# A six-bank ring with paired maxima in place of a seven-bank ring with single maxima, in the second layer's attentions

## The reference

```
def _attn(x, ctx, wq, wk, wv, wo, bo, num_heads):      # 16 heads of 16 columns
    q, k, v = ...                                      # projections
    scores = jnp.einsum('bthd,bshd->bhts', q, k) / np.sqrt(hd)
    p = jax.nn.softmax(scores, axis=-1)
    o = jnp.einsum('bhts,bshd->bthd', p, v)
x = _attn(_ln(x), _ln(x), ...) + x        # self1: 512 keys
x = _ffn(_ln(x), ...) + x
x = _attn(_ln(x), context, ...) + x       # cross1: 1601 keys
x = _ffn(_ln(x), ...) + x
```

## Time and profile before

| | |
|---|---|
| median of 3 runs | 3810.48 us (3810.12 to 3816.46) |
| the profiled execution's own time | 3808.21 us |
| its span | 3806.4 us |
| granted TensorE clock, mean over the span | 0.921 |
| a2, from its first maxima to its last values | about 2454 to 2655 us of the span |
| a3, the same | about 3015 to 3590 us |

### The profile page before, as it was taken

One profiled execution on the slowest core, in us unless ns is written; L12 is line 12 of the kernel. 1 busy time (PEld: TensorE's weight loads), 2 busy tenths in 40 slices (PEclk: granted clock), 3 DMA queues, 4 the chain that ended last, 5 costly groups with the idle time before them and its releaser, 6 DMA issues. The chain is left out here.

```text
span 3806.4 us, 50843 instructions
## 1 busy us (share of the span) xinstructions
PE 3285.1 (86%) x17084; PEld 1868.4 (49%) x17084; DVE 2259.6 (59%) x4090; ACT 1817.3 (48%) x3349; POOL 1081.7 (28%) x538
## 2 busy tenths in 40 slices
PE   7978886899799999999997778598678599999776
PEld 5734443778644444444443566333466344444255
DVE  4356664434266666666663454397444499999333
ACT  4434443444334444444444233177344178888733
POOL 0045653000047777777776000012000000000000
PEclk8978997999889999999998899799799699999888
DMA  5877775999966666666661341233463523222210
GB/s 207 279 182 192 188 191 195 310 326 308 291 159 150 148 149 150 149 150 149 148 150 49 139 155 55 83 119 119 170 193 109 154 90 102 97 88 100 82 67 38
DMA packets 364812, 588.04 MB, mean 154 GB/s; under 512 B 47042, under 2 KB 200226, under 8 KB 363470
## 3 DMA queue, kind: packets, MB, share of 16 engines
q1 hardware_dynamic: 363632, 582.64, 52.1%
q10 hardware_dynamic: 958, 2.62, 0.4%
HBM read 341.51 MB, written 240.88 MB: 153 GB/s over the span
## 5 line engine op out<-in xcount | busy, mean ns | idle before, releaser
L1493 ACT ACTIVATE a_prob<-a_ring 128x512 f32<-128x512 f32 (+1 forms) x1088 | 577.8, 600 | 664.9 <-PE a_ring L1413 624.8
L1517 DVE TENSOR_REDUCE a_blk_max<-a_ring 128x1 f32<-128x402 f32 x1024 | 519.7, 568 | 328.9 <-PE a_ring L1397 328.7
L1092 ACT ACTIVATE a_prob<-a_ring 128x512 f32<-128x512 f32 (+1 forms) x1088 | 582.1, 605 | 97.1 <-PE a_ring L1012 92.5
L1363 POOL TENSOR_TENSOR a_prob_sum<-a_prob,a_prob_sum 128x1024 f32<-128x1024 f32 x256 | 599.4, 2380 | 3.8 <-ACT a_prob L1493 3.8
L1435 PE MATMUL a_pv<-a_prob,a_v 128*64 128x512 f32 (+1 forms) x2176 | 545.4, 621 | 0.0
L1137 DVE TENSOR_REDUCE a_blk_max<-a_ring 128x1 f32<-128x402 f32 x1024 | 507.1, 568 | 63.8 <-PE a_ring L999 57.0
L1412 PE MATMUL a_ring<-a_q_stack,a_k_stack 128*128 128x512 f32 (+1 forms) x1088 | 468.6, 431 | 53.2 <-issue 38.4
L1413 PE MATMUL a_ring<-a_q_second,a_k_second 65*128 65x512 f32 (+1 forms) x1088 | 441.9, 406 | 0.0
L1363 POOL TENSOR_TENSOR a_prob_sum<-a_prob 128x1024 f32<-128x1024 f32 x128 | 301.9, 2369 | 453.6 <-DVE a_chunk_sum L1548 244.2
L1030 PE MATMUL a_pv<-a_prob,a_v 128*32 128x256 f32 (+2 forms) x4096 | 340.7, 406 | 13.6 <-ACT a_prob L1092 7.8
L742 DVE TENSOR_TENSOR p_split_lo<-p_ps,p_split_hi 128x512 fp32r<-128x512 f32 (+2 forms) x280 | 171.4, 622 | 302.6 <-ACT p_split_hi L630 299.8
(11 more groups left out here) (252 smaller groups left out, 4660.0 us busy)
## 6 DMA issues: line engine op xcount, KB each, us to landing
a_k_stack<-k_hi_cross SPq DMA_DIRECT2D x96, 400.5 KB, 4.6
a_v<-v_cross SPq DMA_DIRECT2D x48, 768.0 KB
a_k_stack<-k_lo_cross SPq DMA_DIRECT2D x80, 400.5 KB, 6.0
a_k_second<-k_hi_cross SPq DMA_DIRECT2D x32, 801.0 KB, 12.5
v_cross<-p_v_sb SPq DMA_DIRECT2D x48, 512.0 KB, 4.1
k_hi_cross<-p_split_hi SPq DMA_DIRECT2D x120, 200.0 KB, 3.3
k_lo_cross<-p_split_lo SPq DMA_DIRECT2D x120, 200.0 KB, 3.4
a_q_stack<-q_hi_self SPq DMA_DIRECT2D x64, 256.0 KB, 4.1
```

The source lines that it names most:

```text
L1092: nc.scalar.activation(prob[0:keys, tau % RC, m, :], ring[0:keys, score_place(e) % BANKS, :], ACT.Exp, scale=a.scale).then_inc(exp_done, 1)
L1363: nc.gpsimd.tensor_tensor(prob_sum[:, h], prob_of(i * NCP + cp, h), other, ALU.add)\
L1493: nc.scalar.activation(prob_of(w, h)[0:keys, ch % 2, :], ring[0:keys, score_bank(e), :], ACT.Exp, scale=a.scale).then_inc(exp_done, 1)
L1517: nc.vector.reduce_max(dst, ring[:, max_bank(g), 0:a.blk], AX.X).then_inc(item_read, 1)
```

## The change

VectorE takes both blocks of a pair by one instruction: it reads two neighbouring banks (two runs of 402 or 512 values in each partition) and writes two maxima. It starts when both products have landed, and marks both as read when it ends. For the two banks of a pair to be neighbours wherever the ring has come to, the ring has six banks in place of seven. The eighth bank of PSUM goes to the values as before, and one bank is now unused.

```diff
@@ -773,7 +773,7 @@
-    BANKS = 7
+    BANKS = 6
@@ -1129,13 +1129,14 @@
             def blocks(g0, g1):
-                for g in range(g0, g1):
-                    i, j, t, nb, r = item_of(g)
-                    c = 8 * r + 4 * j + t
-                    dst = blk_max[:, i % 2, c, nb:nb + 1] if NB > 1 else row_max[:, i % 2, c:c + 1]
-                    dve.wait_ge(item_done, g + 1)
-                    nc.vector.reduce_max(dst, ring[:, item_place(g) % BANKS, 0:a.blk], AX.X).then_inc(item_read, 1)
-                    if g % NI == NI - 1:
+                for g in range(g0, g1, 2):
+                    i, j, t, nb, _ = item_of(g)
+                    c, n = 4 * j + t, item_place(g) % BANKS
+                    dst = blk_max[:, i % 2, c:c + 9:8, nb] if NB > 1 else row_max[:, i % 2, c:c + 9:8]
+                    dve.wait_ge(item_done, g + 2)
+                    nc.vector.reduce_max(dst, ring[:, n:n + 2, 0:a.blk], AX.X).then_inc(item_read, 2)
+                    if g % NI == NI - 2:
                         turn(i)
```

## The result

The changed kernel takes 3878.5 us (median of 4 runs, 3871.7 to 3884.75) against 3810.96 for the kernel before on the same chip (3810.12 to 3816.46). The ratio is 1.0174 [1.0154, 1.0194]: slower by 67.5 us where 48 were forecast. The profiled execution took 3879.94 us.

A forecast was written before the change was run, and what follows sets the result against it. It took TensorE as slightly the tighter in a3, with VectorE right beside it, and VectorE as the bound in a2. Terms 50 - 4 + 2 gave 48 us more, 3858 us, range 3834 to 3882.

The forecast's parts named there:

- the walk: Hand timing of ring waits in both attentions; four a3 half-units go from 5.04 to 5.58 us, a2's loop takes 2.73.
- Six banks, a3: In a3's units, maxima and scores wait for banks held by exponentials: 50 us more, bounds 42 and 61.
- VectorE's own part in the ring is no limit in a3: In a3, maxima's banks are free about 1.4 us behind their product, scores need them 2.0 or more behind: no cost.
- Six banks, a2: In a2's units, VectorE stays the bound and the unit goes from 2.87 to 2.91 us: 2 us more.
- the once-a-group work: In a2, VectorE's 1.6 us a group comes in two lumps, of which 0.7 a group sticks out.
- One reduction for two: VectorE's paired reduction takes 983 or 1211 ns, saving 0.067 or 0.069 us a pair; only the starts count, 4 us less.
- the 4 us at the starts: Ahead of each attention's first unit, where only VectorE limits, 42 and 18 pairs save 4 us.
- VectorE's time is what counts: Rival: the ring has room, so less VectorE work speeds both attentions: 34 us less, 3776; faster has chance 0.10.
- TensorE hides the late load: Rival: in a3 the maxima's new wait of 0.38 us costs only 0.07, total 3810; no change has chance 0.04.
- The clock: Rival: stalls draw the clock to 0.50 for a tenth of a3, 50 us on top, 3908; chance 0.05.
- a2's unit was to stay within 0.1 of 2.87 us: Sign in a2: the time per unit should hardly move, staying within 0.1 of 2.87 us.
- The maxima's load was to wait for ScalarE: Sign in a3: the maxima's weight load waits for ScalarE several times the earlier 25.3 us of 480.

The follow-up runs named there:

- e1: Kernel before, with six ring banks in place of seven and single reductions kept: 3876.7 us against 3811.0, ratio 1.017.
- e4: Changed kernel, with ScalarE computing only 256 of 512 columns of each a3 exponential, so the output differs: 3840.1 us (one run).
- e5: Kernel before, with ScalarE computing only 256 of 512 columns of each a3 exponential, so the output differs: 3806.0 us (one run).
- e2: Changed kernel, with seven banks in place of six; pairs whose banks are not neighbours are read by two reductions: 3837.1 us, ratio 1.006.
- e7: Kernel before, but both banks of a pair are marked as read only by the second single reduction: 3843.7 us (one run).
- e6: Kernel before, but the first single reduction of a pair waits for both products: 3812.5 us (one run).
- e9: Changed kernel, with the values of a group's first chunk multiplied in two halves of the columns: 3861.8 us, ratio 1.0127.
- e8: Kernel before, with the values of a group's first chunk multiplied in two halves of the columns: 3807.0 us against 3811.8, ratio 0.9977.
- e10: e8 with paired reductions only ahead of each attention's first unit, seven banks, single ones where the ring wraps: 3803.0 us, ratio 0.9968.

## Why the prediction was right, and where it was not

**The number.** 3878.5 us lies 20 us above the 3858 forecast and near the upper end of the range. The spans differ by 71.8 us, 24 more than forecast, and the traces put 11.5 us of this excess in a2, 2.6 in the starts, 1.8 in a3, and 7.3 ahead of a2, where nothing was changed and only scatter stands. That a3 came so close, 51.8 against 50, is partly luck: the ring alone, which the walk was about, costs 43.8, at the lower end of its 42 to 51, and 8.0 more (e1 to after) came from a step that the prediction had put at nothing.

**Six banks, a3 (predicted +50).** The mechanism held. A round of four half-units that starts with one of two pairs takes 5.58 us in e1 (mean of 32 rounds away from the undivided values) and 5.62 after, where it took 5.07 before; the walk had 5.58 and 5.04. Two plain ones in a row take 2.67 in both, where it had 2.62. The timeline of e1, from a half-unit with two pairs to the next, shows its last step:

```profile
3205.79 0.18 PEld L1012 LDWEIGHTS a_ring<-a_q_stack,a_k_stack 64*128 64x128 f32 x2 [0.41 <-DVE a_blk_max L1137]
...
3207.19 0.51 PEld L1012 LDWEIGHTS a_ring<-a_q_stack,a_k_stack 64*128 64x128 f32 x2 [0.41 <-ACT a_prob L1092]
```

The second load of that row starts 0.18 us ahead of its end, at 3207.52, which is 1.73 us behind 3205.79 as forecast. But the first load, from which half-units are counted, needs only the first exponential and stands at 1.40. So with single reductions those with two pairs take 1.40 and the one behind them 1.54, and not 1.73 and 1.18; the walk had given the whole wait to the first of them. The number of units in 400 us, 141, VectorE's share (84.7%, said 82), ScalarE's (78%) and the clock came as forecast. That this loop hangs on the exponentials is shown by e4 and e5 for the kernel after (27.5 us of 51.8); for e1 alone no run shortened them, and it rests on the row above and the walk.

**The failed step in a3 is "VectorE's own part in the ring is no limit in a3".** It looked at the scores that need the bank of a pair of maxima 2.0 us behind, and overlooked the second pair of maxima of a half-unit with two: with six banks it needs the pair three earlier, and its own slot is only about 1.38 us behind that (1.18 for a half-unit and 0.2 for the first pair). Paired, these banks are free 0.48 + 1.00 + 0.05 = 1.53 us behind their products' start, as in e4's row of 3201.39. In the single form the first bank came back about half a microsecond sooner. With seven banks this is worth 18.1 us (e2), of which e7 gives 13.5 to the late release and e6 1.7, near its scatter, to the late start; the 3 us between them and e2 (the paired start's 0.065 us, the wrap of the ring) were not taken apart. Ring and pairs don't add: 43.8 and 18.1 apart, 51.8 together. That fits delays that overlap, as the half-unit behind one with two pairs takes 1.45 us in e1 and 1.34 after, but no run takes it apart.

**Six banks, a2 (predicted +2, bounds -8 and +14; measured +13.7).** Score products in 120 us fell from 167 to 154, so the unit takes 3.12 us where 2.91 was forecast. The groups of a2 after, 2500 to 2620 us:

```profile
L1138 DVE TENSOR_REDUCE a_row_max<-a_ring 128x2 f32<-128x1024 f32 x78 | 91.3, 1209 | 15.3 <-PE a_ring L999 15.3
...
L1012 PE MATMUL a_ring<-a_q_stack,a_k_stack 64*128 64x512 f32 x154 | 37.4, 481 | 17.7 <-DVE a_row_max L1138 17.7
```

VectorE, which the walk kept as the bound, waits 15.3 us of 120 for products, while the scores' products wait 17.7 for VectorE. That is a loop between the two and not a load on one. The timeline of a2 after shows it:

```profile
2562.36 1.06 PE L1030 MATMUL a_pv<-a_prob,a_v 128*32 128x512 f32 x8
2563.36 0.50 PE L999 MATMUL a_ring<-a_k_stack,a_q_stack 63*128 63x512 f32 x2
2563.69 0.40 PE L1012 MATMUL a_ring<-a_q_stack,a_k_stack 64*128 64x512 f32 x2
2563.93 0.40 PE L999 MATMUL a_ring<-a_k_stack,a_q_stack 63*128 63x512 f32 x2
...
2563.99 2.36 DVE L1138 TENSOR_REDUCE a_row_max<-a_ring 128x2 f32<-128x1024 f32 x2 [0.98 <-PE a_ring L999]
...
2565.27 0.50 PE L1012 MATMUL a_ring<-a_q_stack,a_k_stack 64*128 64x512 f32 x2 [0.94 <-DVE a_row_max L1138]
...
2566.28 0.51 PE L999 MATMUL a_ring<-a_k_stack,a_q_stack 63*128 63x512 f32 x2
...
2566.92 1.23 DVE L1138 TENSOR_REDUCE a_row_max<-a_ring 128x2 f32<-128x1024 f32 x1 [0.57 <-PE a_ring L999]
...
2568.20 0.50 PE L1012 MATMUL a_ring<-a_q_stack,a_k_stack 64*128 64x512 f32 x2 [0.18 <-DVE a_row_max L1138]
...
2569.20 0.51 PE L999 MATMUL a_ring<-a_k_stack,a_q_stack 63*128 63x512 f32 x2
```

The last four rows are the loop in its plain form: a unit's second maxima start at 2566.28, their reduction begins 0.64 us behind and takes 1.23, the next unit's second scores, which need both banks, start 0.05 behind its end (2568.20), and the second maxima of that unit 1.00 behind them (2569.20): 2.92 us. In the trace of after the second scores' load stands 0.05 us behind the end of that reduction in every unit of a group, so this loop, and not VectorE's load, sets the pace of all of a2.

The walk had this loop, but at 2.73 us a unit. **The failed step in a2 is the size of its terms**: it let the reduction begin 0.54 us behind its products, where a paired one begins at 0.63, and it put 0.90 from the second scores to the second maxima, where 1.00 stands once the scores have been waited for. The rest (1.23 for 1.21, and 0.05 for 0.08 from the reduction's end to the scores) cancels. It also placed every chunk's values alike. At a group's first chunk they come undivided, 1.06 us at 2562.36, and behind them stand maxima, scores, maxima and scores with no values between. The last of these scores (2565.27) need the whole first reduction: 2563.99 + 1.21 = 2565.20. They idle for 0.94 us, and so does VectorE afterwards.

A group's four units show what each part is worth. From the one that follows a first chunk's values on they took 3.17, 2.48, 3.11 and 2.82 us before and take 3.81, 2.93, 3.08 and 2.66 now. The loop is longer than the walk's by 0.18 us in each of the four, the undivided values add 0.42 in a group, and the once-a-group work adds 0.40 where 0.7 was forecast. Together that is 0.84 us a group, by estimate 11.6 over 55 units, beside the 11.5 that the forecast was short. e9, which puts values back in between, has 2.91, 2.93, 3.08 and 3.13, the loop without the undivided values, and is 6.2 us shorter.

e1 and e7, each with one half of the cause, have 3.77, 2.87, 3.21 and 2.81. So in a2 either a bank less or a late release is enough for the price, and both together cost no more.

**One reduction for two.** The price was right; these are the paired reductions of a3 and of a2, columns as in the earlier trace rows:

```profile
L1138 DVE TENSOR_REDUCE a_blk_max<-a_ring x512: 952/996/1000, 3036.4 to 3616.6; 128x2 f32<-128x804 f32 x171
L1138 DVE TENSOR_REDUCE a_row_max<-a_ring x128: 1182/1212/1228, 2462.0 to 2654.3; 128x2 f32<-128x1024 f32 x128
```

996 and 1212 ns stand beside a predicted 983 and 1211. VectorE's timeline at both starts, beside the earlier trace rows:

```profile
3036.42 28.96 DVE L1138 TENSOR_REDUCE a_blk_max<-a_ring 128x2 f32<-128x804 f32 x32 [45.56 <-PE a_ring L999]
...
2462.01 9.14 DVE L1138 TENSOR_REDUCE a_row_max<-a_ring 128x2 f32<-128x1024 f32 x8 [32.06 <-PE a_ring L999]
```

(28.96 - 0.99) / 31 is 0.902 us from start to start and (9.14 - 1.21) / 7 is 1.133, where 0.900 and 1.129 were forecast. But of the 4 us at the starts only 1.4 came with six banks, and 2.9 with seven (e2). The fewer banks delay the first scores by themselves: in e1, without pairs, the starts are 0.5 and 0.6 us longer than before.

**The rivals.** "VectorE's time is what counts" is excluded by e2: less of VectorE's work, in a ring as long as before, made the units longer. The rule of the Trainium skill that stood with it (VectorE: DVE Perf Modes, Rules for kernel authors, few operations) held for the price of the instruction and, in this kernel, for the starts; in the units the trace goes against it by 18.1 and 11.5 us. "TensorE hides the late load" would have left a3 where it was, and e1 has 43.8. The clock stayed at 1.00 in the stretches of both attentions.

**The signs that missed.** a2's unit was to stay within 0.1 of 2.87 us and went to 3.12. The maxima's load was to wait for ScalarE for several times 25.3 us of 480, and shows 18.4 of 400. The wait is there, but inside rows of two loads, as in the row of 3206.09: the first load's bank is free, only the second is held, and the idle time of a group counts only what lies ahead of its rows.

## What to carry to other kernels

When two reads of a ring are joined into one instruction, their first buffer comes back later by most of an instruction, and if the ring must shrink for it, by another slot: walk the producer's order slot by slot through the longest period (here a whole group, where one chunk has its values in another place and six half-units have a second pair), and compare, at the tightest place of it, the time from a product to the next use of its buffer with the time until that buffer is given back. An engine that is busy for 97% need not gain from less work when what it reads and what it frees stand in one loop with another engine. Join reads only where nothing waits for the buffers, as at a stage's start, and put work that needs no buffer between the products that do (e8 and e10, both together: 3803.0 us against 3811.8).

## What the runs showed of the hardware

- One reduction over two banks costs 996 ns for 2 x 402 columns and 1212 for 2 x 512, 0.14 to 0.15 us less than two single ones end to end, but only 0.07 less from start to start (0.902 against 2 x 0.4835 us), since single ones overlap each other.
- It begins later behind its products than a single one that also waits for both of them: 0.476 to 0.48 us against 0.412 in a3, 0.630 against 0.564 in a2. Why was not found.
- Waiting for the second product of a pair as well starts a reduction 0.035 us later (0.412 against 0.376, e6) and costs hardly anything; giving back the first bank with the second costs 13.5 us in a3 and 17.7 in a2 (e7).
- A weight load of TensorE that waits for a bank starts 0.04 to 0.05 us behind the end of the instruction that frees it (3201.62 to 3201.66 before, 3201.34 to 3201.39 in e4). In after's a2, maxima follow scores that had waited for a bank by 1.00 us, where 0.90 stood before without a wait.
